# Layer 0 of a graph network: one-hot matrices, shift and self scale moved to GpSimd, and a new order of steps

## The reference, cut to what matters

```python
h = jnp.maximum(_layernorm(x, axis=-1), 0.0)
def sage(h, w_self, w_neigh, b):
    agg = jax.ops.segment_sum(h[src], dst, num_segments=n) * inv_deg
    return h @ w_self + agg @ w_neigh + b
h = jax.nn.relu(sage(h, ws0, wn0, b0))      # 128 -> 256
h = jax.nn.relu(sage(h, ws1, wn1, b1))      # 256 -> 256
x = x + sage(h, ws2, wn2, b2)               # 256 -> 128
```

## Time and profile before

| what | value |
|---|---|
| time, median of 3 runs | 4386.35 us (4383.37 to 4386.78) |
| the profiled execution's own time | 4345.58 us |
| its span in the profile | 4343.4 us |
| mean granted TensorE clock over the span | 0.91 |
| busy over the span: TensorE, VectorE, ScalarE, GpSimd | 83%, 81%, 70%, 52% |
| layer 0 in the profile | from about 133 to 2153 us |

### The profile page before, as it was taken

The page is one execution under the profiler, slowest core; times in us unless marked ns, Lnnn a source line. Parts: engine busy times, 40 slices in busy tenths (PEclk is TensorE's granted clock), DMA queues, the critical chain, the costliest instruction groups (busy, mean ns, idle before and its releaser), DMA issues. The chain is left out here.

```text
span 4343.4 us, 111247 instructions
## 1 busy us (share of the span) xinstructions
PE 3606.9 (83%) x22511; PEld 3214.4 (74%) x22511; DVE 3539.2 (81%) x12507; ACT 3039.1 (70%) x8013; POOL 2257.1 (52%) x2513
## 2 busy tenths in 40 slices
PE   0799999999999999999878888887878766666665
PEld 0688888888888888888777777777777755555555
DVE  8899999999999999999767676666766756666666
ACT  1688888888888888888666666666666656666666
POOL 0444444444444444444355555555555556666665
PEclk9999999999999999999999999999999965555556
DMA  1244444444444444444466666666666677777777
GB/s 50 86 143 142 140 141 143 142 140 141 144 141 139 142 143 140 139 142 143 135 177 193 191 193 194 192 194 189 195 195 194 192 199 219 217 223 218 214 221 207
DMA packets 1040774, 727.06 MB, mean 167 GB/s; under 512 B 103208, under 2 KB 1012656, under 8 KB 1040632
## 3 DMA queue, kind: packets, MB, share of 16 engines
q1 hardware_dynamic: 854298, 569.93, 44.0%
q0 software_dynamic: 80848, 104.93, 10.1%
q10 hardware_dynamic: 105600, 51.92, 4.0%
HBM read 451.60 MB, written 360.71 MB: 187 GB/s over the span
## 5 line engine op out<-in xcount | busy, mean ns | idle before, releaser
L587 POOL DMA_INDIRECT loaded_rows<-in_x,gather_at x784 | 858.4, 1095 | 1048.5 <-ACT h_nbr L694 906.9
L1276 PE MATMUL ps_out<-w_hi,hid_hi 128*128 128x512 f32 (+1 forms) x3136 | 1113.7, 355 | 253.1 <-DVE hid_lo L1169 96.9
L601 POOL DMA_INDIRECT layer_mem<-p_rows,gather_at x784 | 784.8, 1001 | 586.7 <-issue 223.1
L1276 PE MATMUL ps_out<-w_hi,hid_lo 128*128 128x512 f32 (+1 forms) x3136 | 1072.2, 342 | 0.0
L1276 PE MATMUL ps_out<-w_lo,hid_hi 128*128 128x512 f32 (+1 forms) x3136 | 1067.8, 341 | 0.0
L1276 PEld LDWEIGHTS ps_out<-w_hi,hid_hi 128*128 128x128 f32 x3136 | 595.9, 190 | 405.2 <-issue 242.8
L614 POOL DMA_INDIRECT layer_mem<-z_rows,gather_at x528 | 525.8, 996 | 322.3 <-issue 153.2
L1276 PEld LDWEIGHTS ps_out<-w_hi,hid_lo 128*128 128x128 f32 x3136 | 595.3, 190 | 72.8
L1276 PEld LDWEIGHTS ps_out<-w_lo,hid_hi 128*128 128x128 f32 x3136 | 597.8, 191 | 58.4
L1169 DVE SCALAR_TENSOR_TENSOR hid_lo<-ps_out,hid_hi 128x512 fp32r<-128x512 f32 x392 | 270.2, 689 | 400.1 <-ACT hid_hi L777 330.6
L788 ACT ACTIVATE layer_mem<-iota_row,triple_node 128x128 f32<-128x128 f32 x1056 | 347.5, 391 | 259.5 <-issue 178.8
(11 more groups left out here) (163 smaller groups left out, 8933.1 us busy)
## 6 DMA issues: line engine op xcount, KB each, us to landing
p_rows<-stored_rows SPq DMA_DIRECT2D x392, 256.0 KB, 2.2
q_rows<-layer_mem SPq DMA_DIRECT2D x392, 256.0 KB, 2.6
loaded_rows<-q_rows SPq DMA_DIRECT2D x392, 256.0 KB
loaded_rows<-y_rows SPq DMA_DIRECT2D x264, 192.0 KB
layer_mem<-in_x SPq DMA_DIRECT2D x264, 192.0 KB
out_rows<-stored_rows ACTq DMA_DIRECT2D x264, 192.0 KB
loaded_rows<-in_x SPq DMA_DIRECT2D x392, 128.0 KB
z_rows<-layer_mem SPq DMA_DIRECT2D x392, 128.0 KB
```

The source lines that it names most:

```text
L587: pool.indirect_dma_start(raw[s.slot][0:rows, 2 + j, :], None, table, bass.IndirectOffsetOnAxis(gather_at[s.slot][0:rows, j:j + 1], axis=0 ...
L601: pool.indirect_dma_start(rows_in[s.slot][0:SLOT_ROWS, j, 0:width], None, table, bass.IndirectOffsetOnAxis(gather_at[s.slot][0:SLOT_ROWS, ...
L1276: ins = nc.tensor.matmul(o, a, b, start=n == 0, stop=n == len(terms) - 1)
```

## The change

GpSimd makes the one-hot matrices of layer 0 (into buffers of their own, `node_select`), minus the mean, the shift and the self scale, in its step behind the gather. VectorE loses these operations and its step is put in another order: p rows, bn_aggr, degree, agg, the two reciprocals, q rows, `cat_lo`, `hid_lo`. The p and q rows now come six steps behind the pair's entry. `hid_lo` moves from lag six to four, `cat_lo` from four to three, TensorE's output layer from seven to five, ScalarE's h1 and hid_hi from five to four, and the normalisation from the head of the step at lag two to its end at lag one. The lags of SP stay.

```diff
+                    t, u = first.back(2), first.back(3)
+                    if t.live():
+                        if t.has(2):
+                            pool.wait_ge(L0.summed, t.back(2).n + 1)
+                        pool.tensor_tensor(node_now[t.half][:, :], slot_node[:, bass.ds(t.n * 2, 2)], ones[:, 0:2],
+                                           ALU.mult).then_inc(L0.node_copied, 1)
+                        pool.wait_ge(L0.moments_ready, t.n + 1)
+                        pool.tensor_tensor(minus_mean[t.half][:, :], moments[t.half][:, :, 0], minus_ones[:, :], ALU.mult
+                                           ).then_inc(L0.mean_turned, 1)
+                        pool.wait_ge(L0.mean_turned, t.n + 1)
+                        pool.wait_ge(L0.rstd_ready, t.n + 1)
+                        if t.has(2):
+                            pool.wait_ge(L0.normed, t.back(2).n + 1)
+                        pool.tensor_tensor(shift[t.half][:, :], minus_mean[t.half][:, :], rstd[t.half][:, :], ALU.mult
+                                           ).then_inc(L0.shift_ready, 1)
+                    if u.live():
+                        two = bass.ds(u.n * 2, 2)
+                        pool.wait_ge(L0.recip_done, u.n + 1)
+                        if t.live():
+                            pool.wait_ge(L0.node_copied, t.n + 1)
+                        pool.tensor_tensor(self_scale[:, two], inv_degree[:, two], fast[:, :].to_broadcast([P, 2]),
+                                           ALU.mult).then_inc(L0.scale_ready, 1)
...
+                    if t.live():
+                        for j in range(2):
+                            last = pool.tensor_scalar(node_select[t.half][:, j, :], iota_row[:, :],
+                                                      node_now[t.half][:, j:j + 1], None, op0=ALU.is_equal)
+                        last.then_inc(L0.selected, 1)
-                pipeline(pool, step, PAIRS, 1)
+                pipeline(pool, step, PAIRS, 3)
...
             with pool.Else():
+                pool.wait_ge(nodes_made, 1)
                 layer0_gathers(x, SLOT_ROWS)
...
-                    dve.tensor_tensor(select[t.half][:, :, :],
...
-                    dve.tensor_scalar(self_scale[:, two], inv_degree[:, two], fast[:, :], None, op0=ALU.mult
-                                      ).then_inc(L0.scale_ready, 1)
...
-                    dve.scalar_tensor_tensor(shift[t.half][:, :], moments[t.half][:, :, 0], -1.0, rstd[t.half][:, :],
-                                             op0=ALU.mult, op1=ALU.mult).then_inc(L0.shift_ready, 1)
...
-            pipeline(dve, layer0, PAIRS, 8, rounds=3)
+            pipeline(dve, layer0, PAIRS, 6, rounds=3)
...
-                        last = nc.tensor.matmul(ps_agg[:, j * H:j * H + D + 2], select[t.half][:, j, :].bitcast(FP32),
+                        last = nc.tensor.matmul(ps_agg[:, j * H:j * H + D + 2], node_select[t.half][:, j, :],
```

More of the change, by code:

```diff
@@ L210, in build @@
         shift = [sb(f"shift{i}", [P, 4]) for i in range(2)]
+        minus_mean = [sb(f"minus_mean{i}", [P, 4]) for i in range(2)]
         h_own = [sb(f"h_own{i}", [P, 2, D]) for i in range(2)]
@@ L219, in build @@
         gather_at = [sb(f"gather_at{i}", [P, SHARED], I32) for i in range(SLOTS)]
+        node_now = [sb(f"node_now{i}", [P, 2]) for i in range(2)]
+        node_select = [sb(f"node_select{i}", [P, 2, P]) for i in range(2)]
         select = [sb(f"select{i}", [P, 2, P], FP32R) for i in range(2)]
@@ L681, in step @@
                 def step(first):
[L682 to L696, removed]
                     t = first.back(3)
@@ L709, in step @@
                                        ).then_inc(L0.std_ready, 1)
-                    t = first.back(5)
+                    t = first.back(4)
                     if t.live():
@@ L732, in step @@
                                        ).then_inc(L0.h1_hi_ready, 1)
+                    t = first.back(1)
+                    if t.live():
+                        act.wait_ge(L0.shift_ready, t.n + 1)
+                        if t.has(2):
+                            act.wait_ge(L0.summed, t.back(2).n + 1)
+                            act.wait_ge(L0.turned, t.back(2).n + 1)
+                        for j in range(4):
+                            rows = h_own[t.half][:, j, :] if j < 2 else h_nbr[t.half][:, j - 2, 0:D]
+                            if general and j >= 2:
+                                last = act.activation(rows, raw[t.slot][:, j, :], ACT.Copy)
+                            else:
+                                last = act.activation(rows, raw[t.slot][:, j, :], ACT.Relu,
+                                                      bias=shift[t.half][:, j:j + 1], scale=rstd[t.half][:, j:j + 1])
+                        last.then_inc(L0.normed, 1)
                 return step
@@ L1151, in layer0 @@
                                       ALU.add).then_inc(L0.p_ready, 1)
+                if u.live():
+                    for j in range(4):
+                        last = dve.bn_aggr(moments[u.half][:, j, :], stats[u.half][:, j, :])
+                    last.then_inc(L0.moments_ready, 1)
+                s = first.back(2)
+                if s.live():
+                    dve.wait_ge(L0.summed, s.n + 1)
+                    if s.has(2):
+                        dve.wait_ge(L0.turned, s.back(2).n + 1)
+                    two = bass.ds(s.n * 2, 2)
+                    rows = ps_agg[:, :].rearrange("p (j f) -> p j f", j=2)
+                    dve.scalar_tensor_tensor(degree[s.half][:, :], rows[:, :, D], fast[:, :], base_degree[:, two],
+                                             op0=ALU.mult, op1=ALU.add).then_inc(L0.degree_done, 1)
+                    dve.scalar_tensor_tensor(agg[s.half][:, :, 0:D], h_own[s.half][:, :, :], fast[:, :],
+                                             rows[:, :, 0:D], op0=ALU.mult, op1=ALU.add).then_inc(L0.own_added, 1)
+                    dve.wait_ge(L0.degree_done, s.n + 1)
+                    dve.reciprocal(inv_degree[:, two], degree[s.half][:, :]).then_inc(L0.recip_done, 1)
@@ new lines, in layer0 @@
+                if u.live():
+                    dve.wait_ge(L0.std_ready, u.n + 1)
+                    if u.has(2):
+                        dve.wait_ge(L0.normed, u.back(2).n + 1)
+                    dve.reciprocal(rstd[u.half][:, :], std[u.half][:, :]).then_inc(L0.rstd_ready, 1)
+                if t.live():
+                    dve.wait_ge(L0.p_ready, t.n + 1)
+                    dve.wait_ge(L0.scale_ready, t.n + 1)
+                    for j in range(2):
+                        last = dve.scalar_tensor_tensor(q_out[t.slot][:, j, :], p_out[t.slot][:, j, :],
+                                                        self_scale[:, bass.ds(t.n * 2 + j, 1)],
+                                                        ps_out[t.half][:, j * 2 * H + H:(j + 1) * 2 * H],
+                                                        op0=ALU.mult, op1=ALU.add)
+                    last.then_inc(L0.rows_ready, 1)
```

135 lines of the change are left out of this document (52 added, 83 removed).

## The result

The changed kernel takes 4407.97 us, the median of five runs (4404.09 to 4414.57), against 4386.35 before: a ratio of 1.0056, 95% interval 1.0045 to 1.0067. It is slower by 22 us. The forecast was 4384 and no change. The time lies in the wide range of 4375 to 4470, but not because the sum was right: what came true is one of the two slower rivals, at a third of its price.

A forecast was written before the change was run, and what follows sets the result against it. TensorE at 5.107 us a pair was taken to bound layer 0; the moved work and new waits were priced at nothing, fill and drain at -2: 4386.35 - 2 = 4384 us, own range 4380 to 4389, wide range 4375 to 4470.

The forecast's parts named there:

- the two slower rivals: Layer 0's loop: GpSimd becomes the bound (4454 us, chance 0.26), or gathered rows land late (4430 us, chance 0.09).
- What bounds before: Layer 0's steady loop: TensorE sets the step at 5.107 us a pair, VectorE just under it at 5.04.
- VectorE's relief, 5.04 to 4.26: VectorE in layer 0 loses select, self_scale and shift, 0.784 us a pair; worth nothing on the path.
- GpSimd's sum, 4.34: GpSimd's work in layer 0 with the added operations: 4.34 us a pair, 0.77 under the step, bounds 3.36 and 5.38.
- Hold-up by hid_lo: VectorE's hid_lo in layer 0 delays GpSimd: 0.34 us a pair in a rival, 0.49 by the skill's rule.
- GpSimd becomes the bound: Slower rival in layer 0: bigger comparisons and hid_lo's delay make GpSimd 5.28 us a pair, +68, 4454 us; chance 0.26.
- No block grows: TensorE in layer 0 runs its blocks in another order, none of them longer; priced at nothing.
- Round one and round two: Layer 0's two loops of waits through GpSimd must close: 3.83 of 5.107 us, and 9.45 of 10.21 through the gather.
- Fill and drain, -2: Start and end of layer 0's pipeline: output layer joins earlier, first copy and shift later; net -2, bounds -6 and +3.
- comparisons of 0.5 and more: Sign of a wrong forecast: GpSimd's comparisons in layer 0 at 0.5 us or more, where near 0.3 was expected.
- a step other than 5.11: Sign of a wrong forecast: time between aggregations in layer 0 not 5.11 us.
- idle time ahead of ps_agg: Sign of a wrong forecast: TensorE idle before layer 0's aggregation, put down to GpSimd's node_select or ScalarE's h_nbr.

The follow-up runs named there:

- r11: The changed kernel with no further edit, run again on a chip where the kernel before takes 4388 us: 1.0065 of before.
- r10: The changed kernel with no further edit, run on a chip where the kernel before takes 3927 us: 1.0013 of before.
- r2b: The changed kernel with shift and self scale back on VectorE, no minus_mean, rstd earlier in VectorE's order; comparisons stay on GpSimd: 0.9970 of before.
- r3: The changed kernel with the index copy moved from GpSimd to VectorE: 1.0013 of before.
- r7b: The kernel before, its order and lags kept, with node_now, comparisons and self scale moved to GpSimd: 1.0003 of before.
- r9: The changed kernel with hid_lo made from the PSUM sums, without bias and ReLU (a timing probe): 0.9975 of before.
- r1: The changed kernel with the one-hot comparisons back on VectorE as one instruction: 0.9972 of before.
- r16: The kernel before with the changed kernel's new buffers allocated at their places but never used, no instruction changed: 0.9984 of before.
- r15: The changed kernel with hid_lo from PSUM (no bias and ReLU) and one spare GpSimd product, its buffer allocated last: 0.9971 of before.
- r12: The changed kernel with hid_lo from PSUM (no bias and ReLU) and one spare GpSimd product, its buffer allocated ahead of node_select: 1.0021 of before.

## Why it lost more on one kind of chip

The changed kernel was 3 to 4.5 us above before on one kind and 22 to 27 us on the other, with the same busy time of GpSimd (4.66 and 4.67 a pair, operations added up). One long step of the changed kernel, in the profile of the result:

```profile
974.57 0.61 PE L1326 MATMUL ps_agg<-h_nbr,node_select 128*128 128x130 f32 x4
...
974.79 0.37 DVE L1130 BATCH_NORM_AGGREGATE moments<-stats 128x2 f32<-128x6 f32 x4
...
974.98 1.00 POOL L594 DMA_INDIRECT loaded_rows<-in_x,gather_at  x1 [0.30 <-issue]
...
975.34 0.27 PE L1337 MATMUL ps_turn<-ident,layer_mem 128*128 128x128 f32 x1
...
976.52 0.60 ACT L748 ACTIVATE cat_hi<-ps_turn 128x512 fp32r<-128x512 f32 x1 [0.30 <-PE ps_turn L1337]
976.54 0.22 DVE L1140 SCALAR_TENSOR_TENSOR degree<-ps_agg,fast,base_degree 128x2 f32<-128x2 f32 x1 [1.38 <-PE ps_agg L1326]
```

The aggregation ends at 975.18, the last transpose at 975.61. VectorE and ScalarE go on at 976.54 and 976.52, just after the second gather's issue has ended (975.98). In the records of semaphore updates, the signal of the last aggregation matmul comes 1.5 us after that matmul's start and that of the last transpose 1.2 us after its own, where both are 0.29 in before. In the two profiles on this kind of chip (the result's and r11) the transposes' signal comes more than 0.4 us after the matmul's start in 311 of 348 and 312 of 348 steps, and in all but one of these 623 the matmul ended while a gather was being issued. On the other kind of chip r10 has as many such meetings, and all of 380 signals are in time.

The meeting alone is not enough, though. Before, on the chip of the result, has it in nearly every step too: 371 of its 382 last transposes end inside a gather's issue, and not one signal is late. They end in its first 0.1 us (365 of them), and its aggregations in the last 0.2 us of the first gather's issue. The late ones of the changed kernel end 0.25 us or more into the second gather's issue (in that range 304 of 313 are late in the result's profile, 300 of 308 in r11), and the signal mostly comes 0.46 us after the issue's end. In r2b, on the chip of r11, such meetings are rare and 375 of 376 signals are in time. r3, on that chip, has late signals for most of its transposes (203 of the 234 that the record has), some of which end up to 0.3 us behind the issue; that may be the second cause it needed. So on this kind of chip TensorE's signals come late if they fall into a certain part of a gather's issue, by up to 1.1 us, and in the changed kernel they do fall there. These counts show that the two go together. That cat_hi waits 47.0 us for the transposes in the result's profile, and not at all in r10's, fits it. Why the kinds differ, and whether the lateness is all of the 20 us, was not tried.

## Why the prediction was wrong, by its steps

- *What bounds before.* Right: TensorE at 5.107, VectorE beside it. Taking work off VectorE in the old order (r7b) gave nothing.
- *VectorE's relief, 5.04 to 4.26.* Too large. Its records added up fell by 0.75 us a pair, as forecast, but its busy time by 0.49, to 4.56: in before the records overlap each other more. It cost nothing, as VectorE does not set the step.
- *GpSimd's sum, 4.34.* This step failed. The comparisons are 0.61 alone (r9), not 0.30: I sized them by a write of 256 columns, as if reading came free, and the upper bound (0.60) was the value. That is 0.61 more a pair. Small operations at 0.19 measured 0.20, gathers with their gap 2.49 measured 2.41, semaphores at 0.15 measured 0.16 and 0.08. Alone GpSimd's step is 4.72 (r9).
- *Hold-up by hid_lo.* In the prediction it stood in a rival, at 0.34 and at 0.49 a pair; it is 0.35 (r10). The gathers' 1.05 in the mean is not part of it, as they take 1.05 in r9 as well. It belonged in the sum, since the rows for it were there. The full sum is then 4.72 + 0.35 = 5.07, all of TensorE's 5.073. I take it that a step with more hold-up than the mean then gets longer. The sum gives the 5.11 of one kind of chip only nearly, and not the 5.17 of the other; the rest there stays open, with the late signals as the only sign.
- *The rival "GpSimd becomes the bound".* The right mechanism, both of its conditions met. Its 5.28 was 0.2 too high against this sum (neighbouring operations overlap by 0.02 to 0.06 us), and +68 was against a step of 5.107. In place of it stand 5.11 and +3 to +4.5 us on one kind of chip, 5.17 and +22 to +27 on the other.
- *"No block grows".* By starts the output layer's block grew from 2.81 to 2.87 us and the hidden layer's shrank from 1.49 to 1.40 (r1). TensorE's own step fell by 0.034 us, 13 us in all: 0.020 through addresses (r16) and 0.013 that I put down to the order of blocks, which no run shows by itself. A gain that the prediction had no term for hid 13 of some 35 us of loss on the result's kind of chip, and most of the loss on the other.
- *Round one and round two.* They close: r9 keeps the order and all of GpSimd's operations and runs at 5.074. What they did not allow for is a signal that comes up to a microsecond late.
- *Fill and drain, -2.* Right in size: the first aggregation is 2.1 us later, from the last one to layer 1's first gather it is 22.6 instead of 26.4 us, together -1.7.
- *Signs.* Of those named as wrong, "comparisons of 0.5 and more" and "a step other than 5.11" were seen; idle time ahead of ps_agg was not. It fell ahead of ps_hid, for cat_lo.

## What to carry to other kernels

Before an engine with spare time is given work, price each new kind of operation by one that reads and writes as much, and take the upper bound where no row has it: here the one bad size of 0.3 us, twice a pair, used up all the room. Then add what VectorE's operations with two SBUF inputs take from GpSimd, as a term of the sum and not as a risk. A VectorE operation with one input in PSUM took nothing (r9); a form of hid_lo that reads PSUM and keeps bias and ReLU was not tried. Splitting the moves as r2b does, comparisons to GpSimd and small things left on VectorE, keeps both queues under TensorE's step: 0.9970 of before. But r1, with the comparisons on VectorE, is as fast (0.9972), and 0.9984 is to be had by addresses alone (r16), so little of the gain is owed to moving work. And a comparison of two kernels is only clean if their buffers have the same addresses.

## What was not expected of the hardware

- Addresses of buffers that TensorE reads change its step by up to 1%, with the same instructions and no wait: 5.073 and 5.123 (r15, r12), 5.107 and 5.087 (before, r16).
- On two chips, signals of TensorE that fall into the second gather's issue, 0.25 us or more behind its start, come 0.5 to 1.4 us after the matmul's start (the middle one 1.2) and not 0.29. On the chips of the other kind none does.
- VectorE's hid_lo and a comparison on GpSimd shut each other out only in part: the comparison holds hid_lo back for its first 0.2 us of 0.6, hid_lo holds a comparison back to its end.
- A 128-column comparison with a scalar for each partition takes 0.61 us on GpSimd; VectorE makes the two of a pair in 0.41 with one instruction. The Trainium skill (GPSIMD Engine Reference, section on engine selection) calls GpSimd about twice as slow for operations with two inputs and roughly at line rate for one; this one reads one tensor and a column of scalars, and the pair takes three times as long.
- The kernel before differs by 460 us between kinds of chips with the same layer 0; the difference is in layers 1 and 2.
